# A hypergraph layer on one core: the fp32 matmuls of a step gathered in one stretch, and H turned by a DMA

## What is computed

```python
H = (adj != 0)                                # 128 x 128
Dn = 1 / (H @ adj[0])                         # per row, 0 where the sum is 0
Be = 1 / H.sum(axis=0)                        # per column, 0 where the sum is 0
conv = lambda x, W, b: Dn * (H @ (Be * (H.T @ (x @ W.T)))) + b
h = relu(conv(x, W1, b1))                     # 128 x 512
h = layer_norm(h) * gamma + beta
y = conv(h, W2, b2) + x                       # 128 x 256
out = layer_norm(x + y)                       # so 2x + conv(...)
```

## Time and profile before

| | |
|---|---|
| time, median of 3 executions | 299.07 us (298.92 to 299.09) |
| the profiled execution: time, span | 299.96 us, 298.1 us |
| TensorE busy | 287.0 us, 96% of the span |
| TensorE weight loads | 256.1 us, 86% |
| ScalarE, VectorE, GpSimd busy | 208.3, 206.9, 133.9 us |
| TensorE clock granted | 0.992 of full speed |

### The profile page before, as it was taken

The page is one execution under the profiler, slowest core; times in us unless marked ns, Lnnn a source line. Parts: engine busy times, 40 slices in busy tenths (PEclk is TensorE's granted clock), DMA queues, the critical chain, the costliest instruction groups (busy, mean ns, idle before and its releaser), DMA issues.

```text
span 298.1 us, 5867 instructions
## 1 busy us (share of the span) xinstructions
PE 287.0 (96%) x1918; PEld 256.1 (86%) x1918; DVE 206.9 (69%) x587; ACT 208.3 (70%) x621; POOL 133.9 (45%) x163
## 2 busy tenths in 40 slices
PE   6899999999999999999999999999999999999991
PEld 6779889898998979899897989889898989989880
DVE  1674587593958669394957849395875939485884
ACT  3388676868677786858778686877868686747514
POOL 2214453626344361735345173635526263445462
PEclk9999999999999999999999999999999999999996
DMA  6921030502305050320505041130404022010204
GB/s 220 296 73 36 1 108 0 177 1 63 118 0 176 2 177 2 107 72 11 167 1 176 2 145 34 38 104 2 142 3 141 0 62 82 2 70 3 70 0 141
DMA packets 26437, 22.55 MB, mean 76 GB/s; under 512 B 860, under 2 KB 26152, under 8 KB 26408
## 3 DMA queue, kind: packets, MB, share of 16 engines
q1 hardware_dynamic: 26304, 22.15, 23.8%
q10 hardware_dynamic: 104, 0.04, 0.1%
HBM read 13.80 MB, written 8.39 MB: 74 GB/s over the span
## 4 chain that ended last, share of the span: by engine, by line
DVE 33%; POOL 27%; issue 23%; PE 11%; ACT 3%; DMA 2%; DVEq 0%; POOLq 0%; SPq 0%
POOL xb_sb L810 11%; DVE r_lo L613 8%; POOL rstd L803 7%; DVE g_sb L604 7%; DVE bn_sb L647 6%; DVE z_sb L639 6%; POOL rstd L825 5%; PE bank_v L255 4%; POOL r_hi L818 3%; DVE mv_sb L657 2%; DMA w_raw<-in_L_gnn_W_dram 2%; PE bank_v L240 1%; PE bank_s L219 1%; POOL shift L833 1%; DVE mean L660 1%
## 5 line engine op out<-in xcount | busy, mean ns | idle before, releaser
L818 POOL TENSOR_SCALAR r_hi<-r_sb 128x512 fp32r<-128x512 f32 x64 | 48.2, 753 | 84.3 <-ACT r_sb L438 84.3
L263 PE MATMUL bank_g<-w_hi,r_hi 128*128 128x258 f32 x256 | 69.3, 303 | 0.0
L265 PE MATMUL bank_g<-w_lo,r_hi 128*128 128x256 f32 x256 | 63.8, 281 | 0.0
L438 ACT ACTIVATE r_sb<-bank_v,vec 128x512 f32<-128x512 f32 x64 | 44.2, 691 | 15.8 <-PE bank_v L255 15.8
L255 PE MATMUL bank_v<-u_hi,w_hi 128*128 128x512 f32 x128 | 51.9, 406 | 0.4 <-DVE u_lo L573 0.4
L255 PE MATMUL bank_v<-u_lo,w_hi 128*128 128x512 f32 x128 | 50.5, 395 | 0.0
L255 PE MATMUL bank_v<-u_hi,w_lo 128*128 128x512 f32 x128 | 50.5, 394 | 0.0
L265 PEld LDWEIGHTS bank_g<-w_lo,r_hi 128*128 128x128 f32 x256 | 48.4, 189 | 1.0
L263 PEld LDWEIGHTS bank_g<-w_hi,r_hi 128*128 128x128 f32 x256 | 48.3, 189 | 1.1
L613 DVE TENSOR_TENSOR r_lo<-r_sb,r_hi 128x512 fp32r<-128x512 f32 x64 | 47.6, 747 | 1.0 <-POOL r_hi L818 1.0
L270 PE MATMUL bank_g<-w_hi,r_lo 128*128 128x258 f32 x256 | 41.3, 283 | 0.0
(11 more groups left out here) (96 smaller groups left out, 489.3 us busy)
## 6 DMA issues: line engine op xcount, KB each, us to landing
x_sb<-in_x_dram SPq DMA_DIRECT2D x16, 512.0 KB, 3.9
out_dram<-z_sb SPq DMA_DIRECT2D x15, 512.0 KB, 4.6
adj_sb<-in_adj_dram SPq DMA_DIRECT2D x16, 256.0 KB, 5.0
w_raw<-in_L_gnn_W_dram SPq DMA_DIRECT2D x2, 512.0 KB, 5.3
out_dram<-z_sb SPq DMA_DIRECT2D x2, 256.0 KB, 2.6
b_half<-in_L_gnn_b_dram SPq DMA_DIRECT2D x1, 128.0 KB, 7.4
edge_rows<-in_adj_dram ACTq DMA_DIRECT2D x1, 32.0 KB, 3.1
vec_rows<-in_L_gnn_b_dram ACTq DMA_DIRECT2D x1, 2.0 KB
```

Source lines behind the costliest of these rows:

```text
L263: pe.matmul(bank_g[:, n, 0:W2COLS], r_hi[:, i % 2, k, graph(n)], w2_hi[:, k], start=(k == 0), stop=False)
L265: pe.matmul(bank_g[:, n, 0:DOUT], r_hi[:, i % 2, k, graph(n)], w2_lo[:, k], start=False, stop=False, skip_group_check=True)
L438: nc.scalar.activation(r_sb[:, k], bank_v[:, k % 2], ACT.Relu, bias=vec[:, k:k + 1]).then_inc(relu_ready, 1)
L818: nc.gpsimd.tensor_scalar(r_hi[:, i % 2, k], r_sb[:, k], 1.0, 1.0, ALU.mult, ALU.mult).then_inc(r_hi_ready, 1)
```

## The change

The fp32 pieces of a step move to one place behind v3: turned A of group i+2, y of i, u of i+2 (one group further on than before), s of i+3, and the turned squares of i+1. Ahead of them stand all g and v of the step, now as g0, g1, v0, g2, v1, g3, v2, v3. The turned squares of group i+1 are made at the end of step i and go to the bank of g3, so g3 waits until sum_q has read them; turned A of group 1 and later goes to `bank_q`. From group 3 on, H is turned by a DMA from `h_sb` to `turned_h`, issued by SyncE between the load of adj and the load of x, and read_ht reads `turned_h`. The orders of ScalarE, VectorE and GpSimd follow. Cut to its core (the first step and the last are written out apart):

```diff
@@ SyncE
+            def turn_h(j):
+                sp.wait_ge(h_ready, j + 1)
+                if j > ON_PE:
+                    sp.wait_ge(h_dma_turned, 16 * (j - ON_PE))
+                if j >= ON_PE + 2:
+                    sp.wait_ge(ht_ready, j - 1)
+                sp.dma_start_transpose(turned_h[:, j % 2], h_sb[:, j % 2].rearrange("p n c -> p (n c)")).then_inc(
+                    h_dma_turned, 16)
...
             for i in range(G):
                 if i + 6 < G:
                     load_adj(i + 6)
+                if i + 4 < G:
+                    turn_h(i + 4)
                 if i + 3 < G:
                     load_x(i + 3)
@@ TensorE
             def make_g(i, n):
+                if n == PER - 1:
+                    pe.wait_ge(q_summed, i + 1)
...
             def turn_q(i):
                 pe.wait_ge(q_ready, i + 1)
                 pe.wait_ge(q_summed, i)
-                pe.wait_ge(a_ready, min(i + 3, G))
+                pe.wait_ge(g_ready, i * 2)
...
-                make_v(i + 1, 1)
-                if i + 3 < G:
-                    turn_h(i + 3)
-                make_v(i + 1, 2)
-                make_v(i + 1, 3)
+                make_v(i + 1, 2)
+                make_v(i + 1, 3)
                 if i + 2 < G:
                     turn_a(i + 2)
                 make_y(i, 0)
                 make_y(i, 1)
+                if i + 2 < G:
+                    make_u(i + 2)
+                if i + 3 < G:
+                    make_s(i + 3)
+                if i + 1 < LAST:
+                    turn_q(i + 1)
@@ VectorE
-            for i in range(G):
-                if i < LAST:
-                    split_u(i + 1)
+            for i in range(LAST):
+                if i == 0:
+                    add_squares(0)
+                split_u(i + 1)
...
                 if i + 2 < G:
                     make_d(i + 2)
...
+                if i:
+                    if i + 3 < G:
+                        make_b(i + 3)
+                    take_stats2(i - 1, 0)
+                    take_stats2(i - 1, 1)
+                    make_var2(i - 1)
+                    if i + 4 < G:
+                        make_h(i + 4)
+                split_r(i + 1, 0)
                 make_var1(i)
...
+                split_r(i + 1, 1)
+                add_pair(i + 1, 0)
                 read_g(i)
...
                 if i + 1 < LAST:
                     make_z(i, 0)
+                    make_z(i, 1)
+                    add_pair(i + 1, 1)
+                    add_pairs(i + 1)
+                    split_r(i + 1, 2)
                     split_r(i + 1, 3)
@@ GpSimd
                 split_r(i + 1, 0)
-                add_b2(i)
+                split_r(i + 1, 1)
                 inverse_std1(i)
-                split_r(i + 1, 1)
                 split_r(i + 1, 2)
+                if i + 1 < LAST:
+                    add_b2(i + 1)
                 split_r(i + 1, 3)
```

More of the change, by code:

```diff
@@ L188, in _ @@
             load_adj(5)
+            turn_h(3)
             for i in range(G):
@@ L213, in make_s @@
                 pe.wait_ge(wcol_ready, j + 1)
-                if j >= 2:
-                    pe.wait_ge(q_summed, j - 2)
-                else:
+                if j:
                     pe.wait_ge(a_ready, j)
+                    pe.wait_ge(at_ready, j)
                 for n in range(PER):
@@ L225, in turn_a @@
                 for n in range(PER):
-                    mm = pe.transpose(bank_h[:, graph(n)], a_sb[:, n], ident[:, :])
+                    mm = pe.transpose(turned_a[j][:, graph(n)], a_sb[:, n], ident[:, :])
                 mm.then_inc(a_turned, 1)
@@ L340, in _ @@
             turn_a(1)
+            turn_h(2)
             pe.wait_ge(w2_ready, 1)
             for i in range(G):
-                last = i == LAST
                 make_g(i, 0)
[L346 to L351, removed]
                 if i == 0:
@@ L395, in read_ht @@
             def read_ht(j):
-                act.wait_ge(h_turned, j + 1)
+                if j < ON_PE:
+                    act.wait_ge(h_turned, j + 1)
+                else:
+                    act.wait_ge(h_dma_turned, 16 * (j - ON_PE + 1))
                 act.wait_ge(b_ready, j)
@@ L503, in _ @@
             read_at(1)
+            read_ht(2)
             square(0, 0)
             square(0, 1)
-            read_ht(2)
             square(0, 2)
             square(0, 3)
-            make_htb(2)
             for i in range(G):
-                if i < LAST:
-                    split_u(i + 1)
-                if i + 2 < G:
-                    make_a(i + 2)
+                if i == 0:
+                    split_u(1)
+                    make_htb(2)
+                sum_q(i)
                 if i == LAST:
-                    sum_q(i)
+                    normalise(i - 1, 0)
+                    normalise(i - 1, 1)
+                    normalise_last()
+                    break
+                if i + 3 < G:
+                    if i == 0:
+                        relu(1, 0)
+                        square(1, 0)
+                        make_a(2)
+                    read_ht(i + 3)
                 if i:
-                    normalise(i - 1, 0)
-                if i < LAST:
+                    if i + 2 < G:
+                        make_a(i + 2)
+                    if i + 3 < G:
+                        make_htb(i + 3)
                     relu(i + 1, 0)
                     square(i + 1, 0)
-                    sum_q(i)
+                    normalise(i - 1, 0)
+                relu(i + 1, 1)
+                square(i + 1, 1)
+                if i:
+                    normalise(i - 1, 1)
+                else:
+                    make_htb(3)
+                relu(i + 1, 2)
+                square(i + 1, 2)
+                relu(i + 1, 3)
                 if i + 2 < G:
                     read_at(i + 2)
[L526 to L540, removed]
+                square(i + 1, 3)
+                if i + 2 < G:
+                    split_u(i + 2)
         @block.vector
@@ L860, in _ @@
             copy_w(2)
-            for i in range(G):
+            add_b2(0)
+            for i in range(LAST):
                 if i + 3 < G:
                     copy_w(i + 3)
-                if i == LAST:
-                    pool.wait_ge(q_ready, G)
-                    add_b2(i)
-                    break
                 if i:
```

77 lines of the change are left out of this document (41 added, 36 removed).

## The result

The changed kernel takes 302.49 us (median of 6 runs, 302.19 to 303.66) against 299.18 us (median of 6, 298.92 to 300.28) of the kernel before. The ratio is 1.0107, 95% interval 1.0083 to 1.013: slower by 3.3 us, where 303.0 us was predicted.

The account below looks back on a forecast made before the run. TensorE was taken to bound the kernel; the new step, g3's end to the next, summed to 17.44 us for 17.14. Thirteen steps +3.9, last y +1.1, first y -0.7, end -0.4: 299.07 + 3.9 = 303.0 us, range 297.6 to 306.0.

Parts of the forecast that it names:

- The bound and the main wait: TensorE sets the step; after the change y waits for read_g, a 3.55 us chain against 3.21 of cover, 0.34 late.
- The pair waits for GpSimd's power: On VectorE, the first addition of squares, ahead of read_g, waits until GpSimd's power ends: read_g 0.34 us later per step.
- The rival with the free pair: VectorE's first addition of squares does not wait for GpSimd's power: step 17.10, time 298.3 us; chance 0.26.
- The wait of u for z: On TensorE, u behind y waits for make_z and starts cold: 0.2 us per step, bounds 0 and 0.3.
- TensorE's own work: A step's TensorE work without waits falls from 17.14 to about 16.45 us, 0.69 less.
- exits: TensorE's extra cost on leaving fp32 work: 0.47 us per step before, 0.09 after, so 0.38 less.
- entries: TensorE's extra cost on entering fp32 work: 0.07 us each, three go at most, two thirds of them taken.
- The ends: Outside the thirteen steps: last y +1.1 us, first y -0.7, the end -0.4 as the last variance product meets no add_b2.
- H by DMA is hidden: The DMA turning H takes 2 to perhaps 10 us under some 11 us of cover, so it costs nothing.
- r_hi 2: Rival: GpSimd's r_hi 2 goes ahead of VectorE's waiting pair, 0.58 us more in fourteen steps, 311 us; chance 0.07.
- r_hi 1: Rival: GpSimd's r_hi 1, late, meets the variance's small product on VectorE, up to 0.2 us per step, 305.8 us; chance 0.10.
- what the saved work alone gives: Rival: nothing waits anywhere, so only TensorE's saved work counts: 290 us; chance 0.01.

Follow-up runs that it names:

- e2: The changed kernel, but the read-out of g takes the variance and does not wait for GpSimd's power, except in the last group: 297.08 us.
- e5: The changed kernel with GpSimd's power of 15 groups replaced by an addition that streams 400 columns of two inputs: 308.71 us.
- e3: The changed kernel with s moved ahead of u on TensorE, so between y and u: 298.16 us.
- e9: The e7 kernel with GpSimd's addition of b2 for group 1 alone moved back behind the power of group 0: 292.71 us.
- e7: The changed kernel with v1 behind g3, engine orders to suit, b2 added at the head of the step, and s ahead of u: 294.88 us.
- e1: The changed kernel with VectorE's first addition of squares (the pair) moved from ahead of read_g to behind it: 318.79 us.

## Why the prediction came out as it did

**The bound and the main wait: right.** TensorE set the step, and after the change y waits for read_g. The chain from g3's end to y was worked out as 3.55 us without the pair's delay, for a cover of 3.21. It measured 3.55, with a lateness of 0.32 at y for 0.34 and 0.10 for the cold start; e2 removes just this, 0.41 per step.

**The pair waits for GpSimd's power: wrong.** This term of the sum added 0.34 per step, 4.4 us over thirteen. The pair took 0.68 in the middle of the power and read_g started 2.62 behind g3, not 2.96. I had extended two rows on streaming operations to the tiny one. e5 shows that the extension fails at the operation, not at the place: with the streaming addition there the pair does wait, and the step is 0.39 longer. The rival with the free pair had this mechanism right. Its 298.3 us were wrong by the two terms that follow, in the other direction.

**The wait of u for z: right, but too small.** Taken was 0.20; e3 gives 0.35, above my bound of 0.30. z starts 0.31 behind y's first half (110.53; of y's eight matmuls the fifth starts at 110.22), not 0.20; u starts 0.14 behind z's end, not 0.05; and u is then itself 0.07 longer.

**TensorE's own work: mis-sized.** I took 16.45; e9, with nothing left to wait for, has a step of 16.64 (16.63 in e7). The change saves 0.50 per step on TensorE rather than 0.69. By pieces, e9 against the earlier trace rows: all g and v of a step take 11.43 for 11.75, which is 0.32 of the 0.38 that I took off for exits. The fp32 pieces other than turned H take 5.20 for 5.17, where I had 5.09: the turned squares (0.36 for 0.43) and y (1.73 for 1.78) are shorter, but turned A (0.44 for 0.36), now the first of the stretch, and s (0.89 for 0.82) are longer, and u is as before (1.78). So most of the exits vanish, while hardly anything of the entries does.

Together, against the predicted 17.44: -0.34 for the pair, -0.03 at y (0.41 for 0.44), +0.15 at u and +0.19 of own work make 17.41, for 17.38 measured; the pieces are each read to 0.01 or 0.02. A wrong term and two that were too small nearly cancelled: that the step came out within 0.06 us is luck, and not a sign that the parts were right.

**The ends.** The interval to the y of the last full step cost +1.2 for +1.1, but of other parts: the wait of y is 0.86 with its start, where I had 1.2, and u behind it costs the 0.35 of any step. The step ahead of it cost +0.5 where I counted +0.3, since I had let the change save the turned H in thirteen steps and the kernel before has one in only twelve of them. The first y gave back 1.3 for 0.7, the end 0.7 for 0.4. The reason that I gave for the end did not hold. The product of the last variance still meets the last addition of b2 (285.76 to 288.16 on GpSimd) and still takes 0.55 (VectorE):

```profile
287.63 0.55 DVE L619 TENSOR_TENSOR stat<-stat 128x2 f32<-128x2 f32 x1
```

What is gained stands behind it: the second half of the last group's y starts 1.11 behind the first, where it was 1.75. VectorE now has the first half of that group's g read out by about the end of g3 (290.54 for 290.47), and so starts the second variance 0.20 behind g3, not 0.84.

The sum for the profiled executions was +3.9, and they are 2.5 apart. The forecast then took off 0.9, as the profiled execution lay above the median before; after, it lies at the median. This brought the forecast nearer too, and is luck as well.

**H by DMA is hidden: right.** It lands in 2.4 us, at the low end of 2 to 10, and TensorE and ScalarE wait for it nowhere. The Trainium skill (VectorE: DVE Perf Modes, The three transpose paths) gives 1309 ns for one 128 x 128 bf16 block; the estimate of 5.2 us for four, worked out from it, is over twice what the trace has.

**The other rivals.** r_hi 2 did not go ahead of the pair (it starts at 108.20, the pair has ended at 107.93), and r_hi 1 ended at 106.02, just before the variance's product started at 106.10. Without the two waits, e9 has what the saved work alone gives; it is 292.7 us, not 290, since that work is 0.50 per step.

## What to carry to other kernels

Put the cover where the chain is: the change moved work off TensorE (0.50 us per step), but also took v1 out of the stretch between g3 and y, and g from between y and u. The two waits that this exposed cost 0.41 and 0.35 per step, and together they turned the gain into a loss; with either one taken away (e2, e3) the time was below that of the kernel before. For each wait behind a moved piece, compare the chain with what is left under it, and add the restart (here 0.10 for y, 0.07 for u). When two such waits are found, take both away and look again at the first and last step, where an order that is right in the loop (e7) can collide once.

## What the runs showed of the hardware

- GpSimd's power on 128x4 did not hold off VectorE's two-input operation (the pair, 0.68 to 0.69 us in all fifteen whole-group steps), though it takes 1.39 us. An addition of the same length that streams 128x400 does: the pair ended 0.55 us behind it, as it did behind the b2 addition (0.56, e1) and behind r_hi (0.53). The Trainium skill (SBUF — State Buffer, Who interferes with whom) says that a VectorE instruction with two SBUF inputs contends with a GpSimd instruction that reads SBUF, and that the ports they share are an exclusive lock. For the streaming operations the traces agree; for the power they do not, and the measurement decides.
- In the other direction VectorE's operation does lengthen the power. With r_lo started 0.17 us ahead of it, the power takes 1.39 and ends 0.87 behind r_lo's end; with VectorE idle (e9) it takes 1.02. In the first step of the changed kernel the power starts at 37.58, 0.07 ahead of r_lo, and takes 1.03, though r_lo (0.69) and the pair (0.69) run beside it. In these rows it matters which of the two started first. That the power needs its operands only in a short part at its start would fit all of this, but was not tried by itself.
- A matmul behind an idle spell costs more than the spell: y takes 1.83 (e3) for 1.73 (e9), u takes 1.86 for 1.79, at a granted clock of 1.00.
